# One tile's whole-array products in one piece, and x3's gate products dealt out by chunk between the LSTM's steps

## What is computed

```python
def reference(x, cond_1024, ...):
    # L0: weight, scaled per sequence by cond
    # L1: h = tanh(h @ Wh + xW)                       (RNN, 128 steps)
    # L2: x + x @ (base_layer + rank-8 product)       (per sequence)
    # L3: a = xw_t + prev_h @ Wh                      (LSTM, 128 steps)
    #     i, f, o = sigmoid(...); g = tanh(...)
    #     next_c = f * prev_c + i * g; next_h = o * tanh(next_c)
    x = x + _L0_cond_ref(x, cond_1024, L0_cond_weight)
    x = x + _L1_cond_ref(x, cond_1024, L1_cond_Wx, L1_cond_Wh, L1_cond_b)
    x = x + _L2_cond_ref(x, cond_1024, L2_cond_base_layer, ...)
    x = x + _L3_cond_ref(x, cond_1024, L3_cond_Wx, L3_cond_Wh, L3_cond_b)
    return x
```

## Time and profile before

| what | value |
|---|---|
| median of 3 runs | 1182.2 us (1181.23 to 1182.43) |
| the profiled execution's own time | 1180.78 us |
| its span, first to last instruction | 1179.0 us |
| PE busy | 1131.5 us, 96% of the span |
| DVE busy | 894.3 us, 76% |
| ACT busy | 423.4 us, 36% |
| chain of work that ended last | PE 89%, DVE 3%, DMA 2%, ACT 2% |
| PE's waits, the largest by what is waited for | `folded_parts` 9.9 us, once; the w2 loads 7.8 us, 5 times; x3's low part (L759) 5.3 us, once; the LSTM's transposition (L1035) 4.4 us, 6 times; the RNN's low part (L857) 3.7 us, 3 times |
| granted TensorE clock, mean | 0.988 |

### The profile page before, as it was taken

The page is one execution under the profiler, slowest core; times in us unless marked ns, Lnnn a source line. Parts: engine busy times, 40 slices in busy tenths (PEclk is TensorE's granted clock), DMA queues, the critical chain, the costliest instruction groups (busy, mean ns, idle before and its releaser), DMA issues.

```text
span 1179.0 us, 50475 instructions
## 1 busy us (share of the span) xinstructions
PE 1131.5 (96%) x22740; PEld 752.7 (64%) x22740; DVE 894.3 (76%) x2645; ACT 423.4 (36%) x1033; POOL 55.8 (5%) x75
## 2 busy tenths in 40 slices
PE   5777999999999999999999999999999999999996
PEld 3445667766776676677667766766676677667553
DVE  7778777778777777787777777777777777777665
ACT  6774333333333333233333333333333233333221
POOL 0001000000000000000000000000000000000000
PEclk9888999999999999999999999999999999999999
DMA  9990000000000000000000000000000000000000
GB/s 339 405 347 19 21 20 4 21 21 21 21 20 21 3 21 21 21 21 21 21 20 4 21 21 21 20 21 21 3 21 21 21 21 21 11 12 3 11 12 19
DMA packets 24584, 50.98 MB, mean 43 GB/s; under 512 B 4160, under 2 KB 4288, under 8 KB 23344
## 3 DMA queue, kind: packets, MB, share of 16 engines
q1 hardware_dynamic: 24080, 47.56, 11.3%
q10 hardware_dynamic: 288, 0.20, 0.1%
HBM read 39.36 MB, written 8.39 MB: 40 GB/s over the span
## 4 chain that ended last, share of the span: by engine, by line
PE 89%; DVE 3%; DMA 2%; ACT 2%; issue 2%; SPq 1%; POOL 0%; DVEq 0%; ACTq 0%; POOLq 0%
PE ps_gates L1392 28%; PE ps_gates L1384 27%; PE ps_l L1323 14%; PE ps_x L1323 7%; PE ps_rnn L1408 6%; PE ps_rnn L1411 4%; PE ps_z L1323 2%; PE ps_lr L1323 2%; DMA late<-in_base 1%; DMA big<-in_hw 1%; ACT gates_ring L476 1%; SPq L357 1%; PE ps_gates L1294 0%; DVE gates_ring L1013 0%; DVE late L1032 0%
## 5 line engine op out<-in xcount | busy, mean ns | idle before, releaser
L1392 PE MATMUL ps_gates<-big,lstm_h 128*32 128x512 f16 x6144 | 354.4, 379 | 4.4 <-DVE lstm_h L1035 4.4
L1384 PE MATMUL ps_gates<-big,rows 128*32 128x512 f16 x6144 | 344.7, 380 | 5.3 <-DVE rows L759 5.3
L1384 PEld LDWEIGHTS ps_gates<-big,rows 128*32 128x32 f16 x6144 | 164.9, 97 | 173.2 <-issue 7.1
L1392 PEld LDWEIGHTS ps_gates<-big,lstm_h 128*32 128x32 f16 x6144 | 158.1, 97 | 161.7 <-DVE lstm_h L1035 7.3
L600 ACT ACTIVATE gates_ring<-gates_ring 128x256 f32<-128x256 f32 x128 | 53.4, 417 | 343.1 <-DVE gates_ring L1013 343.1
L1013 DVE SCALAR_TENSOR_TENSOR gates_ring<-ps_gates,tile_un,rows 128x256 f32<-128x256 f32 x256 | 111.7, 477 | 79.5 <-PE ps_gates L1392 76.9
L1408 PE MATMUL ps_rnn<-rnn_h,wh_hi 128*128 128x64 f16 x2048 | 120.8, 192 | 3.7 <-DVE rnn_h L857 3.7
L1411 PE MATMUL ps_rnn<-rnn_h,wh_lo 128*128 128x32 f16 x2048 | 116.5, 177 | 0.0
L1408 PEld LDWEIGHTS ps_rnn<-rnn_h,wh_hi 128*128 128x128 f16 x2048 | 93.2, 97 | 34.7 <-issue 28.8
L1411 PEld LDWEIGHTS ps_rnn<-rnn_h,wh_lo 128*128 128x128 f16 x2048 | 91.3, 97 | 0.0
L1032 DVE SCALAR_TENSOR_TENSOR late<-gates_ring,tile_g,cell_tanh 128x128 f16<-128x128 f32 x128 | 45.0, 352 | 60.7 <-ACT cell_tanh L607 60.7
(11 more groups left out here) (182 smaller groups left out, 1536.7 us busy)
## 6 DMA issues: line engine op xcount, KB each, us to landing
ring<-in_hw SPq DMA_DIRECT2D x16, 1024.0 KB, 15.0
...
```

The costliest lines, as they stand in the source:

```text
L1384: nc.tensor.matmul(by_gate(ps_gates[t % 2][B * j:B * j + B, :]), x16[:, part, k, at:at + B], tile_columns(wx3_part(w_part, k), j), start=( ...
L1392: last = nc.tensor.matmul(by_gate(ps_gates[t % 2][B * j:B * j + B, :]), lstm_h16[:, part, k], tile_columns(wh3_part(w_part, k), j), start= ...
```

## The change

Nothing is computed differently; instructions stand in another order on PE, DVE and ACT, and `gates_x` can issue a part of its 12 groups.

- **PE, a pass**: behind `lstm(t)` come all four RNN steps with the whole-array products between them: `rnn(r)`, `z`, `l0`, `rnn(r + 1)`, all of `x3_base`, `x3_low_rank`, `rnn(r + 2)`, `l1`, `rnn(r + 3)`. Then the LSTM's other steps with groups of x3's product between them: `lstm(t + 1)`, 15 groups, `lstm(t + 2)`, 15 groups, `lstm(t + 3)`, 18 groups.
- **`gates_x`** takes a range of its groups, and waits for the high part of x3 ahead of its first group and for the low part ahead of its ninth, where before it waited for the low part ahead of the first.
- **DVE, a pass**: `rnn_out(r)` and `mask_z` stand ahead of the LSTM's transposition; `lstm_out(t)` stands behind `rnn_out(r + 1)`; `x3_first` and `x3_low` stand around `rnn_out(r + 2)`; in the first pass `x_magnitude` stands behind `x3_low`. Behind step t + 1 come `x2`, `tile_scales` and `tile_undo`, behind step t + 2 `xs_low` and `x_magnitude`, behind step t + 3 `x2_low` and `gate_scales`.
- **ACT, a pass**: the RNN's steps first, then the LSTM's t + 1 to t + 3 with `x2_high` and `xs_high` between.
- **The last eight steps** are written out, with x3's groups dealt out between them; the last two `lstm` stand side by side.

```diff
-            def gates_x(t):
+            def gates_x(t, products=range(3 * KC)):
...
-                if t % STEPS == 0:
-                    pe.wait_ge(x3_lo_ready, t // STEPS + 1)
-                wait(pe, gates_ready, 2 * (t - 1))
-                for n, (part, w_part) in enumerate(((0, 0), (0, 1), (1, 0))):
-                    for k in range(KC):
...
+                if products[0] == 0:
+                    wait(pe, gates_ready, 2 * (t - 1))
+                for n in products:
+                    part, w_part, k = n // (2 * KC), n // KC % 2, n % KC
+                    if t % STEPS == 0 and n == 0:
+                        pe.wait_ge(x3_hi_ready, t // STEPS + 1)
+                    if t % STEPS == 0 and n == 2 * KC:
+                        pe.wait_ge(x3_lo_ready, t // STEPS + 1)
...
-                x3_base(a1, (0, 1))
                 rnn(r + 1)
-                lstm(t + 1)
-                gates_x(t + 2)
-                gates_x(t + 3)
-                lstm(t + 2)
+                x3_base(a1, range(KC))
+                x3_low_rank(a1)
                 rnn(r + 2)
-                x3_base(a1, (2, 3))
-                x3_low_rank(a1)
                 if in_l0(i):
                     l1(c)
                 rnn(r + 3)
+                lstm(t + 1)
+                gates_x(t + 2)
+                gates_x(t + 3, range(3))
+                lstm(t + 2)
+                gates_x(t + 3, range(3, 12))
+                gates_x(t + 4, range(6))
                 lstm(t + 3)
-                gates_x(t + 4)
-                if in_rnn(i + 1):
-                    gates_x(t + 5)
-
-            for t in range(T - LAG * STEPS, T):
-                lstm(t)
-                if t + 1 < T:
-                    gates_x(t + 1)
...
+                gates_x(t + 4, range(6, 12))
+                gates_x(t + 5)
+            t = T - LAG * STEPS
+            lstm(t)
+            z(TILES - 1)
+            x3_base(TILES - 1, (0, 1, 2))
+            gates_x(t + 2, range(4))
+            lstm(t + 1)
+            x3_base(TILES - 1, (3,))
+            x3_low_rank(TILES - 1)
+            gates_x(t + 2, range(4, 12))
+            lstm(t + 2)
+            gates_x(t + 3)
+            gates_x(t + 4, range(3))
+            lstm(t + 3)
...
+            lstm(t + 6)
+            lstm(t + 7)
```

67 lines of the change are left out of this document (33 added, 34 removed).

## The result

The changed kernel takes 1184.4 us (median of 10 runs, 1183.5 to 1185.3), the kernel before beside it 1182.2 (10 runs, 1180.5 to 1183.9): a ratio of 1.0019, with a 95% interval of 1.0011 to 1.0027. It is a little slower, by about 2 us. That lies in the predicted range (1178.5 to 1186.2), but the forecast was "no change" with a small gain, and it came out on the other side.

What follows compares the result with a forecast made beforehand. PE's products and the seams between their kinds were taken to bound the kernel. Loop +0.6, first pass +0.5, ahead of the loop -1.3 and the end -1.0 gave -1.2 us: from 1182.2 to 1181.0 us, range 1178.5 to 1186.2.

Steps and rivals of the forecast that it cites:

- pass 31 and the last steps: From lstm(116) to lstm(127): 74.58 us instead of 75.55, so -1.0 us (-0.5 to -1.3), RNN waits included.
- POOL's `xs`: In later passes it starts at T + 3.2 and ends at 4.45, within the RNN's reserve of 0.45 us: no loss.
- the first pass: In pass 2, xs lies beside DVE's x2 and scales without slack and holds an instruction: +0.5 us once (0 to 1.27).
- What bounds the kernel: In the loop PE never stands; a pass of 34.05 us is its products plus the cost of changing kinds.
- rival D: In the loop, no seam is spared because 0.10 and 0.07 us return at the LSTM's waits: 1185.9 us, chance 0.06.
- The LSTM's floor: In the LSTM's steps, the chain of 3.32 us plus lstm's 2.60 allows no step under 5.92 us.
- rival B: In the loop the LSTM's chain is shorter than at the end, 15 groups cover it: 1175.5 us, chance 0.10.
- The second step: From lstm(t + 2) to lstm(t + 3), DVE with x2 and six scale instructions is 0.02 to 0.09 us late; 0.02 taken.
- rival C: In the loop, POOL's xs lands on the RNN's chain if starting behind T + 3.65: slower, 1192.6 us at halfway, chance 0.10.
- Ahead of the loop: Before lstm(0), x3's first 8 groups start about 2.05 us earlier on its high part: -1.3 us, between -1.6 and -1.0.
- four of 5.92: In the last steps, four LSTM steps of 5.92 us each, the last all chain between lstm(126) and lstm(127).
- the same: For the whole kernel, a time not distinguishable from no change, 1179.8 to 1184.6 us: chance 0.60.

Runs made afterwards that it cites:

- the first experiment: Changed kernel with PE's order in pass 31 altered, x3_base halves and x3 groups filling the RNN waits: single time 1182.5 us, lstm(116) to lstm(121) 37.84 instead of 40.23.
- the second: Changed kernel with x3's last groups dealt out otherwise, gates_x(127) between the last two lstm: 1185.0 us, the step 5.93 instead of 6.36 us.

## Why the prediction was right or wrong

The sum had -1.2 us and the kernel became 2.2 us slower. Its part behind `lstm(0)`, +0.1 (+0.6, +0.5 and -1.0), came out at +4.2, its part ahead of it, -1.3, at -1.7 to -2.4. That the median still lies in the range is in part luck: the two errors have opposite signs. What turned the sign is the term for pass 31 and the last steps, which left out the clock and the bank; POOL's `xs` and the first pass added to it. Step by step:

**What bounds the kernel: right.** PE's products and the seams between their kinds make a pass. The whole-array part without a wait is 15.697 us; with the steps of 5.926, 5.981 and 6.485 a pass has 34.09. Without the LSTM's waits (5.84 for a step of 2.60 and 15 groups) it would be 33.86, 0.19 under before. The seams were sized at 0.17, and rival D falls.

**The LSTM's floor: right, its size a little low.** 5.92 forecast, 5.926 measured, 5.925 with 13 groups: rival B falls.

**The second step: the term was mis-sized.** The forecast had 5.94 (0.02 us late, and 0.09 as its other end) and took the lower end, because a pair of rows showed an overlap of 0.08 us. The overlap is there (`x2` to its follower 0.60 us), but the six small instructions and the way from the last of them to the sums take 1.24 us, not 1.19. It cost 0.04 us a pass, 1.1 us in 28; moving the scales gave back 0.05.

**POOL's `xs`: the step that failed in kind.** The forecast worked out a start at T + 3.2 and set a point at T + 3.65 from which rival C begins, and then held that "the distance of 7.97 us hardly varies". It varies, and the trace of before shows it already: over its passes it runs from 7.90 to 8.68 us, 8.2 on average, and the row of 7.97 is one of the short ones. In the changed kernel `xs` started between T + 3.1 and T + 4.1, and the passes in which it came late pay 0.04 to 0.4 us. The point from which it costs lies at T + 3.87 and not at T + 3.65, so the reserve was larger than worked out, which kept the loss small. Rival C was no case of its own with a chance of 0.10, but a part of the forecast, 0.3 to 1.3 us in the sum in four traces (three of after, one of it with the single wait). Passes of 34.09 throughout, once the reduction stood earlier, show it.

**The first pass: mis-sized.** +0.5 forecast as what the nearest row held, +1.0 to +1.2 measured in four traces. Both held instructions, on 128 x 128 and on 128 x 2 elements, let their followers start 0.06 to 0.07 us behind the end of `xs`. The rule of the Trainium skill (SBUF — State Buffer, Who interferes with whom), that a DVE instruction with two SBUF inputs and a GpSimd instruction that reads SBUF block each other for the whole of the one that came first, agrees with this trace nearly to the end of `xs`: 1.03 us lost of the 1.17 left, 0.63 of 0.77 in the later pass. By it the forecast had 1.1 for this pass.

**Ahead of the loop: right in kind, mis-sized.** -1.3 forecast, -2.4 to -2.5 measured in medians, -1.7 as the mean over the starts of `lstm(0)` in all traces. The two cases that it weighed, the clock rising as long behind the new start or at the old moment, were cases of one favourable trace. In the pair of timed runs all of the shift of the start comes through, 2.2 to 2.4 us. The time ahead of the loop varies from one execution of the same kernel to the next by 1.5 us, and the sum was made against one execution. Its statement that the median lies 1.4 us above that execution was right, but it carried the difference over to the kernel after, whose own first trace lay 0.1 us under its median.

**Pass 31 and the last steps: the term that turned the sign.** -1.0 forecast, +1.0 to +1.3 measured in four traces. The RNN's two waits are as worked out (`rnn(r + 3)` starts 13.0 us behind `lstm(116)`, as forecast). Missed were the clock that they let fall (1.4 us, gone with the first experiment) and the wait for the bank behind `lstm(125)` (0.43, gone with the second), a place which the forecast had as one of "four of 5.92". It had the figure for it: it put the end of the sums that free a bank about 1.2 us behind an `lstm`, and three groups are only 0.65 us; it weighed this for the loop and not for the last steps.

**The sum.** Loop behind the first pass +1.5 to +2.4, first pass +1.0 to +1.2, pass 31 and the last steps +1.0 to +1.3, together +4.2 on average over the four traces (three of after, one with the single wait); the split wait -2.4, or -1.7 by the traces. That leaves +1.8 to +2.5, and +2.2 was measured. The clock's fall at the 3.15 us gap ahead of `lstm(127)` is not in this sum: of nine traces with the gap three show it, at 1.3 to 2.5 us, 0.6 on average over the nine. How often it happens in the timed runs was not measured, and a rest of this size stays open.

**The chances.** 0.60 stood on "the same", with the median under 1184.6. The medians, 1184.4 and 1184.2, are just inside that, but the difference is clear of the noise: both timings put it at 0.2%, with intervals (1.0011 to 1.0027, 1.0011 to 1.0030) that leave out 1.
